# Attention of a small language model: the split of the low-rank rows moved to slot 12 of the preceding turn, and the front of the next group moved to slots 0 to 4

## The reference

```python
h = base_weight[x] + einsum('bsr,dr->bsd', lora_A.T[x], lora_B)   # rank 16, width 512
xn = (h - mean(h)) / sqrt(var(h) + 1e-5)
cq, ckv = layernorm(xn @ W_dq) * g + b, layernorm(xn @ W_dkv) * g + b   # 128 columns each
q, k, v = cq @ W_uq, (ckv @ W_ukv)[..., :512], (ckv @ W_ukv)[..., 512:]
p = softmax(causal(q @ k.T / sqrt(32)))                            # 16 heads of 32
h = h + (p @ v) @ W_o.T
h = h + ffn(layernorm(h))                                           # 16 experts, 8 of them per token
```

## Time and profile before

| | before |
|---|---|
| median of 3 runs | 2719.15 us (2715.58 to 2721.16) |
| the profiled execution | 2717.76 us, span 2715.9 us |
| mean granted TensorE clock | 0.988 of full speed |
| PE busy | 2541.1 us (94%) |
| DVE, ACT, POOL busy | 1724.4 (63%), 1838.5 (68%), 1126.7 us (41%) |

### The profile page before, as it was taken

The page is one execution under the profiler, slowest core; times in us unless marked ns, Lnnn a source line. Parts: engine busy times, 40 slices in busy tenths (PEclk is TensorE's granted clock), DMA queues, the critical chain, the costliest instruction groups (busy, mean ns, idle before and its releaser), DMA issues.

```text
span 2715.9 us, 49409 instructions
## 1 busy us (share of the span) xinstructions
PE 2541.1 (94%) x13120; PEld 1883.0 (69%) x13120; DVE 1724.4 (63%) x3742; ACT 1838.5 (68%) x4597; POOL 1126.7 (41%) x1275
## 2 busy tenths in 40 slices
PE   3899999999999999969999999999999999999999
PEld 2566666666666666547878777877877787787787
DVE  5666666666666666357656765765576576557655
ACT  2666666666666666557766866876686677668666
POOL 3433333333333333214444544544464454436445
PEclk8999999999999999979999999999999999999999
DMA  3121212121211111142221222122122213212221
GB/s 100 32 64 62 62 62 63 62 62 62 62 62 62 62 62 46 45 146 90 98 87 50 94 86 86 47 98 86 52 92 88 84 46 100 85 53 89 89 69 60
DMA packets 99807, 197.67 MB, mean 73 GB/s; under 512 B 10928, under 2 KB 10928, under 8 KB 99568
## 3 DMA queue, kind: packets, MB, share of 16 engines
q1 hardware_dynamic: 94576, 179.29, 19.6%
q0 software_dynamic: 5120, 17.31, 2.8%
HBM read 128.89 MB, written 34.08 MB: 60 GB/s over the span
## 4 chain that ended last, share of the span: by engine, by line
issue 28%; POOL 24%; PE 2%; DVE 1%; ACT 1%; POOLq 1%; DMA 0%; SPq 0%; DVEq 0%; ACTq 0%
POOL t_lo L1147 22%; POOL sh_lo L1147 1%; POOLq L1145 1%; DVE ps_u L1516 0%; DVE f_lo L1541 0%; ACT x L1310 0%; DVE t L1523 0%; DMA x<-h 0%; ACT t_hi L1365 0%; PE fwork L1162 0%; PE ps_g L1162 0%; PE ps_u L1164 0%; PE ps_g L1164 0%; PE ps_u L1162 0%; PE ps_y L1162 0%
## 5 line engine op out<-in xcount | busy, mean ns | idle before, releaser
L1147 POOL TENSOR_TENSOR t_lo<-t,t_hi 128x512 fp32r<-128x512 f32 x512 | 664.6, 1298 | 437.2 <-ACT t_hi L1365 437.1
L377 POOL TENSOR_TENSOR probs<-probs,inv 128x512 f32<-128x512 f32 x256 | 265.3, 1041 | 626.6 <-DVE inv L774 626.4
L599 ACT ACTIVATE probs<-ps_s,nmax 128x128 f32<-128x128 f32 x1024 | 363.6, 371 | 222.4 <-DVE nmax L769 222.3
L1516 DVE TENSOR_TENSOR ps_u<-ps_u,square 128x512 f32<-128x512 f32 x512 | 357.3, 698 | 179.5 <-ACT square L1352 142.2
L1365 ACT ACTIVATE t_hi<-t 128x512 fp32r<-128x512 f32 x512 | 320.8, 627 | 129.4 <-PE ps_y L1164 72.6
L1523 DVE TENSOR_TENSOR t<-ps_u,w_all 128x512 f32<-128x512 f32 x512 | 354.0, 691 | 54.2 <-DVE ps_u L1516 18.4
L1348 ACT ACTIVATE square<-ps_g 128x512 f32<-128x512 f32 x544 | 320.5, 589 | 91.7 <-PE ps_g L1164 89.6
L1352 ACT ACTIVATE square<-square 128x512 f32<-128x512 f32 x544 | 344.4, 633 | 17.3
L488 PE MATMUL ps_s<-k_diag,qT 128*128 128x512 f32 x512 | 264.0, 597 | 0.0
L769 DVE TENSOR_REDUCE nmax<-ps_s 128x4 f32<-128x512 f32 x256 | 176.1, 688 | 102.3 <-PE ps_s L488 100.8
L1162 PE MATMUL ps_y<-t_hi,f_hi 128*128 128x512 f32 x512 | 209.9, 410 | 21.9 <-POOL t_lo L1147 21.6
(11 more groups left out here) (196 smaller groups left out, 5519.5 us busy)
## 6 DMA issues: line engine op xcount, KB each, us to landing
w_all<-w_rows SPq DMA_DIRECT2D x256, 256.0 KB, 3.2
res_next<-h SPq DMA_DIRECT2D x64, 256.0 KB, 2.3
res<-res_next SPq DMA_DIRECT2D x64, 256.0 KB, 2.3
h<-res SPq DMA_DIRECT2D x64, 256.0 KB, 2.0
x<-h SPq DMA_DIRECT2D x16, 1024.0 KB, 5.8
fres<-h SPq DMA_DIRECT2D x16, 1024.0 KB, 7.7
out<-fres SPq DMA_DIRECT2D x64, 256.0 KB, 2.3
fres<-in_w_ffn SPq DMA_DIRECT2D x14, 512.0 KB, 3.6
```

The source lines that it names most:

```text
L377: pool.tensor_tensor(probs[:, s % 4, :, :], probs[:, s % 4, :, :], inv[:, s % 4, :].rearrange("p (h o) -> p h o", o=1).to_broadcast([P, HP ...
L599: e = act.activation(probs[:, s % 4, j, :], ps_s[:, s % 2, j, :], ACT.Exp, bias=nmax[:, s % 4, j:j + 1], accum_out=total[:, s % 4, j:j + 1])
L1147: pool.tensor_tensor(lo, t[:, t_slot(j), :], hi.bitcast(F32), ALU.subtract).then_inc(t_lo_done, 1)
L1516: dve.tensor_tensor(dst, product, square[:, j % 2, :], ALU.mult).then_inc(t1_done, 1)
```

## The change

It moves instructions in every engine's queue but SP's, and adds or removes none in a full turn:
- the split of `ar` for group n + 1 goes from slot 0 of turn n to slot 12 of turn n - 1 (that for group 0 stands ahead of turn -1);
- the transposes of `ar` go from the end of slot 0 and the middle of slot 1 to the middle of slot 0, ahead of transposes -2 of the probabilities; in slot 0 DVE and ACT read them ahead of the row maximum and the exponentials;
- the four uses `h` go from slots 1, 1, 2, 3 to slots 0, 1, 1, 2;
- statistics go from slots 2 and 3 to 1 and 2, the Newton steps from 4 to 3, the normalisation from 5 to 4, and the gather from 5 to 4.

```diff
-MIDWAY = {1: (("art", 1), ("h", 0), ("h", 1)), 2: (("h", 2), ("v", 0)), 3: (("h", 3), ("q", 2)),
+MIDWAY = {0: (("art", 0), ("art", 1)), 1: (("h", 1),), 2: (("v", 0), ("h", 3)), 3: (("q", 2),),
           4: (("v", 2),), 5: (("v", 3),), 7: (("out", 0), ("xt", 3)), 8: (("out", 1),),
...
-END = {0: (("k", 1), ("art", 0)), 1: (("q", 1),), 2: (("v", 1),), 3: (("k", 2),),
+END = {0: (("k", 1), ("h", 0)), 1: (("q", 1), ("h", 2)), 2: (("v", 1),), 3: (("k", 2),),
...
-STATS_AT, NORM_AT, C_NORM_AT = (2, 3), 5, 10
+STATS_AT, NORM_AT, C_NORM_AT, SPLIT_AT = (1, 2), 4, 10, 12
...
-GATHER_AT, RSTD_AT, C_RSTD_AT = 5, 4, 9
+GATHER_AT, RSTD_AT, C_RSTD_AT = 4, 3, 9
...
+                    if step == 0:
+                        read_work(n, MIDWAY[step], SOON + LATER)
                     if has_slot(n, step):
                         row_max(n, step)
-                    read_work(n, MIDWAY.get(step, ()), SOON + LATER)
+                    if step > 0:
+                        read_work(n, MIDWAY.get(step, ()), SOON + LATER)
...
-                        if step == 0:
-                            split_ar(n + 1)
+                        if step == SPLIT_AT and not is_turn(n, GROUPS - 2):
+                            split_ar(n + 2)
...
             dve.wait_ge(loaded, 16)
+            split_ar(0)
             turn(-1)
             turn(0)
-            with dve.Fori(1, GROUPS - 1) as n:
+            with dve.Fori(1, GROUPS - 2) as n:
                 turn(n)
-            turn(GROUPS - 1)
-            turn(GROUPS)
+            for n in range(GROUPS - 2, GROUPS + 1):
+                turn(n)
```

More of the change, by code:

```diff
@@ L641, in turn @@
                         o_hi(n, O_HI_AT[step])
+                    if step == 0:
+                        read_work(n, MIDWAY[step])
                     if has_slot(n, step):
                         exps(n, step)
-                    read_work(n, MIDWAY.get(step, ()))
+                    if step > 0:
+                        read_work(n, MIDWAY.get(step, ()))
                     if has_slot(n, step - T_LAG):
```

## The result

The changed kernel takes 2810.19 us (median of 4 runs, 2805.74 to 2820.36), the kernel before 2717.36 in the runs beside it: a ratio of 1.035 (95% interval 1.0319 to 1.0381). Slower was forecast, 2774 with a range to 2798; it is 36 us more than that, and outside the range.

A forecast was written before the change was run, and what follows sets the result against it. PE was taken to bound attention; a turn would gain 0.7 + 1.9 + 1.6 = 4.2 us, over 13 turns 55 us, giving 2774 against the median of 2719.15, with a range of 2742 to 2798.

The forecast's parts named there:

- Turn 14 ... ends about even; the expert phase is unchanged: Last attention turn without a gather, and the experts after it: neither was given any change in time.
- The sum of a turn: Attention turn: 0.7 us for early slots, 1.9 for POOL's chain, 1.6 for a clock fall, together 4.2 us.
- the walk through the banks of slots 0 to 3: Attention, slots 0 to 3: waits for drains of work's two banks make scores 3 start 0.7 us later.
- POOL's chain: Attention, scores 3 to transposes 4: gather ahead of product 4 makes it 14.9 us instead of 13.0, +1.9.
- The wait before transposes 4: Attention, slot 6: PE waits 2.7 us a turn for POOL's product 4.
- The falls of the clock: Attention: PE's clock falls to 0.50 behind the 2.7 us wait, once in each of 13 turns, 1.6 us each.
- The clock stays: Rival for attention: PE's clock stays at 2.4 GHz; 13 x 2.6 = 34 us, so 2753; chance 0.22.
- The early slots keep their gain: Rival for attention: scores 3 starts 2.1 us earlier, paying for POOL's 1.9; 2712 to 2720 us; chance 0.10.
- Two falls a turn: Rival for attention: two clock falls a turn, or one twice as long; 2800 us; chance 0.08.
- the waits that the split had set: Attention, slots 0 and 1: PE's waits of 1.36 and 0.54 us at the transposes of ar, expected to be saved.
- The gather beside xn: Attention: POOL's first transfer beside the last xn takes 1.05 us, the next 0.95, so 0.1 us extra.

The follow-up runs named there:

- e1: The kernel before with one more turn peeled off DVE's attention loop, no operation changed; 2760.25 us, ratio 1.0169.
- e5: The changed kernel with 15 more idle instructions (already satisfied waits) ahead of DVE's expert loop; 2749.52 us, ratio 1.011.
- e9: The kernel before with one more turn peeled off DVE's attention loop and idle waits padded ahead of its expert loop; 2705.36 us, ratio 0.9955.
- e3: The changed kernel with the gather back in slot 5, behind product 4; 2771.93 us, ratio 1.0207.
- e4: The kernel before with the split alone moved to slot 12 of the preceding turn, plus an unused extra gather; 2726.45 us, ratio 1.0034.
- e8: The kernel before with the gather alone moved from slot 5 to slot 4; 2850.67 us, ratio 1.0484.
- e7: The kernel before with DVE's loop over the expert groups written out; 2700.64 us, ratio 0.993.
- e2: The changed kernel with the peeled turn back in DVE's attention loop, plus an unused extra gather and split; 2772.05 us, ratio 1.0204.

## Why the prediction was wrong

**"Turn 14 ... ends about even; the expert phase is unchanged": this is the step that failed.** The expert phase took 53.4 us more. The last lines of the quoted diff, one turn fewer in DVE's loop and one more written out, have no term in the prediction: the phase was put at nothing because no line of it differs. e1, e5 and e9 show that they carried the larger half of the loss. What the runs showed instead is a stop of 3 to 4 us a group, set by the place of DVE's code, which costs 43 us by itself in e1. The warning was in the trace of before: its expert loop stops 2.8 us at each branch and its attention loop doesn't, so the place of the code already had a price there. No row of the instructions brings this up unless one asks for the distance from a branch to what follows, or for the times of the packets of q14.

**The sum of a turn.** 0.7 + 1.9 was forecast without a fall; 2.47 was measured. Counted from scores 14 of the turn before (664.55 before, 689.41 after), scores 3 starts 0.5 us later, so the walk through the banks of slots 0 to 3 held, and POOL's chain came out at 14.91 against 14.9. e3 shows this cause by itself: with the gather behind product 4, the turn is 68.8. The wait before transposes 4 was forecast as 2.7 and is 2.32. The waits have the names that were forecast: k1's drain, v0's, v3's, and product 4.

**The falls of the clock** were the term of the sum that was mis-sized. Each costs 1.4 to 1.8 us (forecast 1.6), but they come in 7 of the turns, not in 13. A wait of 2.32 us in one turn brings the clock down and the same wait in the next doesn't (724.49 and 796.89 above), so the length of the wait before it doesn't decide by itself; what does was not tried. With 7 falls attention's loss is 43 and not 55; added to before's profiled execution that makes 2761, inside the range. So the range failed by the expert phase alone.

**The rivals.** *The clock stays* is half true, since it stays in about half the turns. *The early slots keep their gain* is refuted by 0.5 us later instead of 2.1 earlier. e4 gives a part of why: behind the waits that the split had set, 1.90 us, stood a bank's drain of 1.57. *Two falls a turn* never appeared.

**The gather beside xn.** The first transfer takes 1.05 and the next 0.95 as in the earlier trace rows. The prediction put this 0.1 down to the `xn` beside it. e3 has the same 1.05 with DVE idle (its next instruction starts at 700.40):

```profile
699.29 1.05 POOL L362 DMA_INDIRECT gath<-in_table,tok_now  x1 [0.84 <-POOL tok_now L359]
```

So the 0.1 belongs to being first, and these transfers show no held port. The index copy does take longer beside the `xn`: 0.38 us at 717.35 and in the earlier trace rows, 0.18 in e3 and e8, where none runs.

## What to carry to other kernels

Peeling or unrolling a loop on one engine moves the code of all its later loops; compare the number of instructions ahead of each loop, measure from each loop's branch to the next instruction, and look whether the instruction queue has packets in the steady passes, before calling a phase unchanged. A loop whose branch costs microseconds can be had cheaper by a few idle instructions ahead of it or by writing it out, here 12 us (e9, where a turn is peeled as well) and 17 us (e7). A wait that names one engine may hide a second of nearly the same length, so moving the named work gains little until both are gone. A stop of the fetch can stand under any engine's name, as in e2.

## What the runs showed of the hardware

- VectorE's code came in packets of 8 KB, one for every 128 instructions (e7: 121 to 138 between two packets).
- A loop of 286 rows whose pass ran into a fourth such block stopped at its branch for 2.8 us or more and had five packets in each pass; one that ended 39 instructions into the third passed it in 0.3 and had none. What happens between these two places wasn't tried.
- VectorE went on 1.8 to 2.2 us after the start of the packet that it waited for, at the branch and at the first border behind it.
- The second packet of a pass started 5.3 to 7.1 us behind the branch. A border 6 instructions behind the loop's head met this with 3.2 to 4.6 us of standing, one at 16 with 0 to 1.4, and those at 21 and 26 with none. The operation that shows the stop has nothing to do with it.
- TensorE's granted clock fell in the groups of the kernels with the long second stop alone: from the third group to the last mark 8 falls in the changed kernel, 5 in e3 and 4 in e1, and none in the nine others.
- ScalarE (261 rows a pass), GpSimd, TensorE and SyncE passed their taken branches in 0.3 us or less in the same phase; only VectorE's loop stood badly.
- GpSimd's index copy took 0.38 us beside VectorE's four normalisations and 0.18 without them.
